# Gate logits of an expert router taken from eight extra columns of a shared-expert up tile, in a fused four-layer kernel

## The reference

```python
logits = x @ gate_weight.T                       # 8 experts
scores = jax.nn.softmax(logits, axis=-1)
topk_w, topk_idx = jax.lax.top_k(scores, 2)
combine = zeros.at[arange(T)[:, None], topk_idx].add(topk_w)
gu = jnp.einsum('th,efh->tef', x, gate_up_weights)      # F = 352
act = jax.nn.silu(gu[..., :F]) * gu[..., F:]
y = jnp.einsum('tef,te,ehf->th', act, combine, down_weights)
sgu = x @ shared_gate_up.T                       # shared expert, Fs = 704
sact = jax.nn.silu(sgu[:, :Fs]) * sgu[:, Fs:]
y = y + sact @ shared_down.T
```

## Time and profile before

| | us |
|---|---|
| median of 3 runs | 3185.6 |
| profiled execution | 3191.16 |
| its span | 3189.4 |
| TensorE recorded busy | 2948.7 (92%) |
| VectorE, ScalarE, GpSimd busy | 1892.3, 1204.9, 615.3 |
| mean granted clock of TensorE | 0.954 |

### The profile page before, as it was taken

One profiled execution on the slowest core, in us unless ns is written; L12 is line 12 of the kernel. 1 busy time (PEld: TensorE's weight loads), 2 busy tenths in 40 slices (PEclk: granted clock), 3 DMA queues, 4 the chain that ended last, 5 costly groups with the idle time before them and its releaser, 6 DMA issues. The chain is left out here.

```text
span 3189.4 us, 42203 instructions
## 1 busy us (share of the span) xinstructions
PE 2948.7 (92%) x13274; PEld 1663.8 (52%) x13275; DVE 1892.3 (59%) x4735; ACT 1204.9 (38%) x2191; POOL 615.3 (19%) x756
## 2 busy tenths in 40 slices
PE   7899979997999678999999999999999999999788
PEld 3344444444556345666556655666556665554333
DVE  5766741000111276777786777777787678737576
ACT  3545510001122145444543555445544445322232
POOL 1111203101111212122312222122222223110000
PEclk9999978998999889999999999999999999999899
DMA  3000142003222451001100011000110001226213
GB/s 119 27 13 28 40 178 96 20 13 125 66 66 65 153 225 69 1 28 54 41 28 15 28 51 45 26 16 28 47 48 14 29 28 41 71 84 239 73 43 92
DMA packets 74816, 197.06 MB, mean 62 GB/s; under 512 B 11376, under 2 KB 12032, under 8 KB 67968
## 3 DMA queue, kind: packets, MB, share of 16 engines
q1 hardware_dynamic: 54992, 149.41, 13.0%
q0 software_dynamic: 9264, 28.36, 2.8%
q10 hardware_dynamic: 10368, 16.83, 1.4%
HBM read 137.90 MB, written 56.66 MB: 61 GB/s over the span
## 5 line engine op out<-in xcount | busy, mean ns | idle before, releaser
L2043 DVE SCALAR_TENSOR_TENSOR c_conv<-c_ps_pj,c_conv_t,c_conv 128x511 f32<-128x511 f32 (+2 forms) x495 | 368.0, 746 | 88.2 <-ACT c_conv L1880 76.5
L1655 PE MATMUL c_ps_pj<-c_w_g,c_xs 128*128 128x512 f32 x512 | 227.6, 592 | 0.0
L1638 PE MATMUL c_ps_pj<-c_xs,c_w_v 128*128 128x512 f32 x480 | 225.8, 593 | 0.0
L1638 PE MATMUL c_ps_pj<-c_xs,c_w_k 128*128 128x512 f32 x480 | 216.0, 593 | 1.1 <-DMA c_xs<-xt_d 1.1
L1638 PE MATMUL c_ps_pj<-c_xs,c_w_q 128*128 128x512 f32 x360 | 193.5, 671 | 2.3 <-DVE c_conv L2043 2.1
L1880 ACT ACTIVATE c_conv<-c_ps_pj,c_conv_t 128x512 f32<-128x512 f32 x165 | 127.9, 775 | 90.0 <-PE c_ps_pj L1638 85.3
L999 DVE TENSOR_TENSOR x_act<-x_hs,x_ps_u 128x352 f32<-128x352 f32 x40 | 20.9, 521 | 226.9 <-ACT x_hs L984 226.9
L2062 DVE TENSOR_TENSOR c_block_X<-c_block_X,c_block_t 128x126 f32<-128x126 f32 (+22 forms) x496 | 139.9, 282 | 18.5 <-DVE c_block_t L2058 1.7
L1655 PEld LDWEIGHTS c_ps_pj<-c_w_g,c_xs 128*128 128x128 f32 x512 | 94.8, 190 | 107.1 <-issue 107.1
L2058 DVE TENSOR_TENSOR c_block_t<-c_block_L,c_block_X 128x126 f32<-128x126 f32 (+22 forms) x496 | 135.3, 273 | 17.0
L852 DVE TENSOR_TENSOR b_act<-b_hs,b_ps_u 128x512 f32<-128x512 f32 (+1 forms) x24 | 16.5, 686 | 205.9 <-PE b_ps_u L744 205.9
(11 more groups left out here) (486 smaller groups left out, 6097.9 us busy)
## 6 DMA issues: line engine op xcount, KB each, us to landing
c_xs<-xt_d SPq DMA_DIRECT2D x16, 1024.0 KB, 4.8
ot_d<-c_oT ACTq DMA_DIRECT2D x64, 256.0 KB, 2.0
b_w_gu<-in_w_gu SPq DMA_DIRECT2D x8, 1408.0 KB, 24.4
y_slots<-x_y SPq DMA_DIRECT2D x40, 256.0 KB, 2.0
a_x<-in_x SPq DMA_DIRECT2D x8, 1024.0 KB, 6.6
d_x<-x SPq DMA_DIRECT2D x32, 256.0 KB, 2.9
d_switch<-in_switch_w SPq DMA_DIRECT2D x4, 2048.0 KB, 17.7
x_w_dn<-in_w_dn SPq DMA_DIRECT2D x8, 768.0 KB, 11.1
```

Of the source, the lines that this page charges most:

```text
L1638: mm = e.matmul(bank_of[xb][u][:, :], w["kqv"[u // HG]][:, k, (u % HG) * DH:(u % HG + 1) * DH], xs[xb][:, k, :], start=(k == 0), stop=(k = ...
L1655: mm = e.matmul(pj[(xb + i) % 2][:, :], xs[xb][:, k, i * P:(i + 1) * P], w["g"][:, k, :], start=(k == 0), stop=(k == KD - 1))
L2043: e.scalar_tensor_tensor(oc, bank_of[buf][u][:, 0:SEQ - s], conv_t[buf][:, m, h, TAPS - 1 - s:TAPS - s], oc, ALU.mult, ALU.add).then_inc(c ...
```

## The change

The gate weights become eight more columns of the third tile (f = 2, called GATED, 96 columns wide) of the first half's up weights, so that rows 96 to 103 of u_ps hold the logits of 512 tokens, by expert. The tile with them is made for all four batches first. ScalarE copies the eight rows to gate_rows, and TensorE turns them with four transposes a batch into the same PSUM bank as before. Two more tiles of batch 0 lie between these transposes. The routing arithmetic follows on VectorE as before, with two tiles of batch 0 made on TensorE ahead of the count products, and one behind them; after that each batch has five tiles and its down products, with all loops but SP's and POOL's written out. The results of the GATED tiles have a place of their own in act (slot).

The weights of the first half with the gate's columns, s_gu0, are loaded by SP in phase_ssm, after the last x of the first pass. The second half, s_gu1, comes first in SP's program of the new phase. ScalarE loads its tables three times in the phase, for silu, for Exp and for silu.

```diff
                 e.dma_start(x[:, :, :], rows(io["x"], b)).then_inc(x_loaded, 16)
+            e.dma_start(s_gu0[:, :, 0:2 * FE], io["w_gu"][NE]).then_inc(shared_loaded, 16)
+            e.dma_start(s_gu0[:, :, 2 * FE:2 * FE + NE], io["gate_w"]).then_inc(shared_loaded, 16)
...
+        s_gu1, s_dn = sb("s_gu1", [P, KD, 2 * FE]), sb("s_dn", [P, NSH, len(FT), DM])
         hs = [sb(f"hs{i}", [P, SEQ]) for i in range(2)]
-        act = sb("act", [P, NF, SEQ])
+        act = sb("act", [P, NF + NB - 1, SEQ])
+        gate_rows = sb("gate_rows", [NE, NB, SEQ])
...
+        s_gu_loaded, s_dn_loaded = sem("s_gu_loaded"), sem("s_dn_loaded")
+        rows_copied = sem("rows_copied")
+        GATED = len(FT) - 1
+        GW = FT[GATED][1]
+        others = [f for f in range(NF) if f != GATED]
+        tiles_of = [(b, GATED) for b in range(NB)] + [(b, f) for b in range(NB) for f in others]
+        of_batch = lambda b, lo=0, hi=NF - 1: range(NB + (NF - 1) * b + lo, NB + (NF - 1) * b + hi)
+        slot = lambda b, f: NF + b - 1 if f == GATED and b > 0 else f
         prefer_made, routing_made = sem("prefer_made"), sem("routing_made")
         logits_ready, counts_ready = sem("logits_ready"), sem("counts_ready")
...
         def _(e):
-            e.dma_start(gate_w[:, :, :], io["gate_w"]).then_inc(gate_loaded, 16)
+            e.dma_start(s_gu1[:, :, :], io["w_gu"][NE + 1]).then_inc(s_gu_loaded, 16)
             for i in range(NSH):
-                e.dma_start(s_gu[:, i], io["w_gu"][NE + i]).then_inc(s_loaded, 16)
-                e.dma_start(s_dn[:, i], io["w_dn"][NE + i]).then_inc(s_loaded, 16)
...
-            e.wait_ge(gate_loaded, 16)
-            for b in range(NB):
-                for c in range(TPB):
+            def gate_logits(b):
+                e.wait_ge(rows_copied, b + 1)
+                for c in range(TPB):
+                    mm = e.transpose(logits[:, b * TPB + c, :], gate_rows[:, b, c * P:(c + 1) * P], con["ident"][0:NE, 0:NE])
+                if b == NB - 1:
+                    mm.then_inc(logits_ready, 1)
+
...
+            def up(s):
+                b, f = tiles_of[s]
+                lo, width = FT[f % len(FT)]
+                s_gu = s_gu0 if f < len(FT) else s_gu1
+                e.wait_ge(act_done, s + 1)
+                if 2 <= s < NB + 2:
+                    e.wait_ge(rows_copied, s - 1)
+                for dst, col, ready in ((g_ps, lo, g_ready), (u_ps, FE + lo, u_ready)):
+                    n = width + NE if f == GATED and dst is u_ps else width
                     for k in range(KD):
-                        mm = e.matmul(logits[:, b * TPB + c, :], XT[:, b, k, c * P:(c + 1) * P], gate_w[:, k, :],
+                        mm = e.matmul(dst[s % 2][0:n, :], s_gu[:, k, col:col + n], XT[:, b, k, :],
                                       start=(k == 0), stop=(k == KD - 1))
-            mm.then_inc(logits_ready, 1)
-
-            e.wait_ge(chosen, 1)
-            for dst, mask in ((earlier, "before"), (in_tile, "ones")):
-                mm = e.matmul(dst, con[mask][:, :], t["key"][:, :, :], start=True, stop=True)
-            mm.then_inc(counts_ready, 1)
-            e.wait_ge(s_loaded, 16 * 2 * NSH)
-            with e.Fori(0, NB) as b:
-                for f in range(NF):
-                    i, (lo, width) = f // len(FT), FT[f % len(FT)]
-                    e.wait_ge(act_done, NF * b + f + 1)
-                    for dst, col, ready in ((g_ps, lo, g_ready), (u_ps, FE + lo, u_ready)):
-                        for k in range(KD):
-                            mm = e.matmul(dst[f % 2][0:width, :], s_gu[:, i, k, col:col + width], XT[:, b, k, :],
-                                          start=(k == 0), stop=(k == KD - 1))
-                        mm.then_inc(ready, 1)
...
+            def down(b, c, f):
+                i, width = f // len(FT), FT[f % len(FT)][1]
+                return e.matmul(y_ps[c][:, :], act[0:width, slot(b, f), c * P:(c + 1) * P], s_dn[0:width, i, f % len(FT), :],
+                                start=(f == GATED), stop=(f == NF - 1))
...
+            for s in range(NB + 2):
+                up(s)
+                if s >= 2:
+                    gate_logits(s - 2)
+            e.wait_ge(s_gu_loaded, 16)
+            for s in of_batch(0, 2, 4):
+                up(s)
+            counts()
+            for s in of_batch(0, 4):
+                up(s)
+            e.wait_ge(s_dn_loaded, 16 * NSH)
+            e.wait_ge(psum_read, 1)
+            downs(0)
+            for b in range(1, NB):
+                for s in of_batch(b):
+                    up(s)
+                downs(b)

...
+            def silus(of):
+                for s in of:
+                    f = tiles_of[s][1]
+                    width = FT[f % len(FT)][1]
+                    e.wait_ge(g_ready, s + 1)
+                    e.activation(hs[s % 2][0:width, :], g_ps[s % 2][0:width, :], ACT.Silu).then_inc(silu_done, 1)
+                    if f == GATED:
+                        e.wait_ge(u_ready, s + 1)
+                        e.activation(gate_rows[:, s, :], u_ps[s % 2][GW:GW + NE, :], ACT.Copy).then_inc(rows_copied, 1)
...
+            e.preload_act_table_set("silu_and_others")
+            silus(range(NB + 2))
+            e.preload_act_table_set("exp_and_others")
             e.wait_ge(route, 3)
             e.activation(t["score"][:, :, :], t["score"][:, :, :], ACT.Exp).then_inc(route, 1)
             e.preload_act_table_set("silu_and_others")
-            with e.Fori(0, NB) as b:
-                for f in range(NF):
+            silus(of_batch(0, 2))
+            copies(0)
+            for b in range(1, NB):
+                silus(of_batch(b))
+                copies(b)
+
...
+            acts(range(NB + 2))
             e.wait_ge(prefer_made, NE + 2)
             e.wait_ge(logits_ready, 1)
...
@@ -796,6 +854,7 @@
                 return m

             m = of_choice(rt.weight, t["score"][:, :, :], m)
+            acts(of_batch(0, 2, 4))

             e.wait_ge(counts_ready, 1)
             e.tensor_copy(count[:, :, :], in_tile.rearrange("p n x -> p x n")).then_inc(route, 1)
@@ -819,6 +878,7 @@
                                    ALU.mult, ALU.add).then_inc(route, 1)
             e.wait_ge(route, m + 9)
             e.tensor_tensor(t["score"][:, :, :], slot_of[:, :, :].rearrange("p x n -> p n x"), earlier, ALU.add).then_inc(psum_read, 1)
+            acts(of_batch(0, 4))
             e.wait_ge(psum_read, 1)
```

More of the change, by code:

```diff
@@ L215, in _ @@
             e.wait_ge(xn_stored, 16 * NB)
+            e.wait_ge(shared_loaded, 16 * 2)
         @block.gpsimd
@@ L724, in _, with counts @@
         def _(e):
-            e.wait_ge(gate_loaded, 16)
-            for b in range(NB):
+            def gate_logits(b):
+                e.wait_ge(rows_copied, b + 1)
                 for c in range(TPB):
+                    mm = e.transpose(logits[:, b * TPB + c, :], gate_rows[:, b, c * P:(c + 1) * P], con["ident"][0:NE, 0:NE])
+                if b == NB - 1:
+                    mm.then_inc(logits_ready, 1)
+            def counts():
+                e.wait_ge(chosen, 1)
+                for dst, mask in ((earlier, "before"), (in_tile, "ones")):
+                    mm = e.matmul(dst, con[mask][:, :], t["key"][:, :, :], start=True, stop=True)
+                mm.then_inc(counts_ready, 1)
@@ L755, in _, with downs @@
+                    mm.then_inc(ready, 1)
+            def down(b, c, f):
+                i, width = f // len(FT), FT[f % len(FT)][1]
+                return e.matmul(y_ps[c][:, :], act[0:width, slot(b, f), c * P:(c + 1) * P], s_dn[0:width, i, f % len(FT), :],
+                                start=(f == GATED), stop=(f == NF - 1))
+            def downs(b):
+                acts_before = 2 + of_batch(b)[-1]
+                e.wait_ge(act_done, acts_before)
                 for c in range(TPB):
@@ L756, in _ @@
                     e.wait_ge(y_copied, TPB * b + c + 1)
-                    for f in range(NF - 1):
-                        down(c, f)
-                e.wait_ge(act_done, NF * b + NF + 2)
+                    for f in [GATED] + others[:-1]:
+                        down(b, c, f)
+                e.wait_ge(act_done, acts_before + 1)
                 for c in range(TPB):
-                    down(c, NF - 1).then_inc(y_ready, 1)
+                    down(b, c, NF - 1).then_inc(y_ready, 1)
+            for s in range(NB + 2):
+                up(s)
+                if s >= 2:
+                    gate_logits(s - 2)
@@ L773, in _, with copies @@
+            def copies(b):
                 for c in range(TPB):
@@ L776, in _, with acts @@
                     e.activation(y[c % 2][:, :], y_ps[c][:, :], ACT.Copy).then_inc(y_copied, 1)
+            e.preload_act_table_set("silu_and_others")
+            silus(range(NB + 2))
+            e.preload_act_table_set("exp_and_others")
+            e.wait_ge(route, 3)
+            e.activation(t["score"][:, :, :], t["score"][:, :, :], ACT.Exp).then_inc(route, 1)
```

(24 more changed lines are left out.)

32 lines of the change are left out of this document (5 added, 27 removed).

## The result

| | before | after |
|---|---|---|
| median of the runs side by side | 3186.71 us (4 runs) | 3156.15 us (4 runs, 3153.95 to 3165.07) |
| ratio, 95% interval | | 0.9912, 0.9899 to 0.9926 |
| mean of all runs, two throttled ones of the kernel before left out | 3184.3 us (44 runs) | 3161.6 us (16 runs) |
| profiled execution, span | 3191.16, 3189.4 us | 3165.07, 3163.3 us |
| mean granted clock | 0.954 | 0.957 |

The kernel is faster, well beyond its measurement's uncertainty. Two later series of the same kernel gave 0.9938 (0.9921 to 0.9955) and 0.9935 (0.9918 to 0.9952), so over all 16 runs the gain is 22.6 us, less than the 30.6 of the first series. The shared-expert phase, from SP's first issue in it to SP's first issue of the next, gained more than either: it took 291.1 us (455.26 to 746.32) and takes 256.1 (456.37 to 712.50), that is -34.9.

A forecast was written before the change was run, and what follows sets the result against it. The prediction took TensorE to bound the shared-expert phase, but for the gap between gate product and counts. Terms -36.8 + 0.6 + 2.4 + 0.5 = -33.3 us gave 3152.3 us from the median 3185.6, range 3147 to 3160.

The forecast's parts named there:

- Start, -36.8: Shared-expert phase start: TensorE begins an up tile at POOL's memset, 455.7, removing everything to 492.52; -36.8 us, ends -37.3 and -34.2.
- Clock, +0.6: First up tile: the clock's rise after idling costs 2.2 us, +0.6 over before; ends 0 and +1.6.
- Eight more columns, 0: u product of the GATED tile: 104 columns in place of 96 cost nothing.
- Transposes, +2.4: TensorE between up tiles: sixteen small transposes at 0.15 us each add 2.4 us; ends 1.7 and 4.4.
- Counts, +0.5: TensorE between two up tiles: the count products return at full clock, adding 0.5 us, between 0.4 and 0.8.
- What hides the rest: Shared-expert phase: routing, copies, token list and loads hide beside TensorE's work; routing slack 5 us, token list slack 100.
- All later phases only shift: Behind the shared-expert phase: its end is as before, so later phases merely start sooner, adding nothing.
- Rival D's second half: Later phases: a longer idle stretch or lower clock from the shifted timing takes part of the gain; 3170 us, 2%.
- A sign that was no sign: State-space phase: as a sign of being right, its time was to equal that of before to 0.5 us.
- Rival A: Shared-expert phase start: TensorE isn't ready at the barrier and starts at 458.3, so the gain is 30.7; 3155 us, 7%.
- B: Up tiles: the routing chain stalls TensorE before tile 8 or the down products; 3158 us, 4%.
- C: First six up tiles: transposes between them keep the clock at 1.2 GHz, a net +5.7 us; 3191 us, 2%.

The follow-up runs named there:

- e8: The kernel before, with 21 tiny copies added on ScalarE ahead of its shared loop, moving all its code behind: 3183.44 us, ratio to before 1.0002.
- e3: The kernel before, with only the gate weights and the first half's up weights loaded early, in the state-space phase: 3177.2 us, shared-expert phase 288.9.
- e10: The kernel before, unaltered, run again for a second usable trace: 3187.27 us, shared-expert phase 292.3.
- e1: The changed kernel once more, unaltered, with a trace: 3164.76 us, ratio to before 0.9938.
- e4: The changed kernel, with four output buffers y for the copied down products in place of two: 3159.38 us, ratio to before 0.9928.
- e5: The changed kernel, with the old 128-record gate product ahead of the first tile in place of extra columns, copies and transposes: 3183.32 us, phase 282.2.
- e7: The changed kernel, with gate weights and the first half's up weights loaded at the start of the shared-expert phase, not early: 3171.52 us, phase 264.3.
- e6: The changed kernel, with the old gate product in place of extra columns and transposes, placed behind the first two up tiles: 3189.04 us, phase 279.8.
- e11: The kernel before, padded in its shared-expert phase on TensorE, VectorE and ScalarE to the changed kernel's program lengths: 3258.37 us, ratio to before 1.0229.
- e9: The changed kernel, with 60 tiny copies added on ScalarE behind the silus of batches 1 to 3: 3161.64 us, ratio to before 0.9936.

## Why the prediction was right, step by step

The predicted 3152 us was 4 below the first series' median, inside the range of 3147 to 3160, but 9.6 below the mean of all 16 runs, 3161.6, just outside it. The three series of the changed kernel have means of 3157.8, 3163.9 and 3161.9 us, so that the first came nearest is in part luck. The range itself was added up wrongly: the worst end of 3158 widened by the spread of 3.9 is 3162, not 3160. The mechanism in the phase was right; what was not is the sentence behind the sum.

- **Start, -36.8.** The bound of -37.3 was nearer: TensorE starts 0.11 us behind SP, not with POOL's memset at +0.47. By SP's first issue it is 492.52 - 455.26 - 0.11 = -37.15.
- **Clock, +0.6.** Measured nothing: the first g records took 5.14 us, before 5.16. The expert phase of the earlier trace rows was a poorer model than before's own first tile. But the records vary by the execution, and alike in both kernels: 5.02 (e8), 6.00 (e3) and 6.02 (e10) with the old start, 5.12 (e1) to 6.26 (e4) with the new one.
- **Eight more columns, 0.** 3.60 us for 104 columns as for 96.
- **Transposes, +2.4.** Measured 7.31 + 7.37 + 7.41 + 7.40 - 4 x 6.87 = +2.0, 0.13 each, some 0.09 of it between the transposes' and the next tile's starts and the rest in the longer g behind them (3.70). The Trainium skill's 275 ns for a 128x128 transpose, measured there in bf16 ("TensorE: Matmul & The Clock Gate", Part 4: PE-mode transpose), had given an estimate of 4.4 us; the measurement decides against it for these small ones in float32.
- **Counts, +0.5.** Measured 0.44.
- **Sum, -33.3.** Now -37.15 + 2.0 + 0.44 = -34.7, measured -34.9. e3, e5 and the changed kernel split it another way: -2.2 for the gate weights on hand (288.9), -6.6 for the choice beside up tiles (282.2), -26.1 for the product itself (256.1). Each comes from single traces, in which the first tile's clock alone moves a phase by 1 us.
- **What hides the rest.** The choice was there 7.7 us ahead of its use, the read-out 3.8 us; e7 prices the early load's cover at 8.2 us, 1.0 of it the clock's. The token list's load was issued at 608.56, for a forecast of 610.
- **"All later phases only shift."** This failed. The expert and output phases did, but of 34.9 us some 12 come back outside, most of it with 23 us more at half clock. Rival D's second half comes nearest to it (a lower clock later out of the shifted timing, 3170) and had 2%, far too little: the delta-rule phase alone varies from 1452.8 to 1459.0 us between the traces of before and its variants and from 1458.3 to 1465.9 between those of the changed kernel, and it was treated as fixed. That the clock is lower because of the shifted timing is not shown.
- **A sign that was no sign.** The state-space phase was to be equal to 0.5 us and was 1.1 longer. From trace to trace it varies from 450.4 to 457.1, whatever the kernel.

Rival A is excluded by e3 and by the trace after, B by the list of waits. What C feared was seen with other work: in e6 the clock fell during the product of eight-column matmuls. With the sixteen transposes amid tiles of 512 columns it stood at 1.00 from 460 on.

So the sum was right for the phase, and the base under it, all other time unchanged, was not. A phase that loses 38 us at half clock should raise the mean clock of the run by 0.006. It rose by 0.003 in the trace and by 0.002 on the mean of the runs, so the gap could be seen in the table of the result.

## What to carry to other kernels

A product of very short matmuls can cost far more than its columns suggest: here 128 records of 8 columns took 0.215 us each at half clock, where transposes of 128 columns took 0.28 each. Where its operand is already streamed by a wide product, a few more columns of that product's weights can be free, as 104 for 96 were here, and transposes of the small result cost 0.13 us each. Compare the phase and the whole apart, and the half-clock time with them: here a third of the gain in one phase did not reach the whole, most of it lost to time at a lower clock elsewhere, and only many runs showed it.

## What the runs showed of the hardware that was not expected

- Through 128 records with eight moving columns, recorded as busy almost without a gap, the clock stayed at 1.2 GHz in before, e3 and e5, all 27.5 us of it. In e6 it was at 2.4 GHz when they began, fell during them and stayed down to their end. At 2.4 GHz they took 0.10 us each (20 in 473 to 475 us), at 1.2 GHz 0.215.
- 625 instructions on TensorE that only wait on a semaphore, almost all of them when it was already there, held it up by 67 us, 0.11 each, at a granted clock of 0.50 (e11).
- Moving code by 625 instructions on TensorE, 20 on VectorE and 29 on ScalarE, as the change and e11 do, moves unexplained waits in a later loop from one engine or place to another: 14.3 us on VectorE, 12 to 15 on TensorE, 13.9 on ScalarE. Taking away ScalarE's (60 more instructions, e9) made no difference that the runs could tell.
- One execution of the kernel before took 8327.46 us (e2), another 13351.43. Two stretches of the first:

```profile
1000.00:2000.00 1000.00, 971.78 (x758) 306.97 (x757) 117.02 (x285) 69.26 (x110) 53.60 (x101) 0.92 0.07 27
3000.00:7000.00 4000.00, 3928.20 (x8836) 2058.14 (x8835) 1194.05 (x2937) 759.20 (x1391) 413.31 (x472) 0.36 0.05 20
```

Over the whole of it VectorE's busy time was 1910.1 us, for 1892.3 in before, ScalarE's 1225.5 for 1204.9, and TensorE's 8157.3 for 2948.7: of the engines, TensorE alone was slowed much.
